# Selective scan: GpSimd's four products in slots 0, 3, 6 and 9 of a group, and the next group's preparation in other slots

## What is computed

```python
xz = x @ W_in
x_inner, z = jnp.split(xz, 2, axis=-1)
xc = jax.lax.conv_general_dilated(x_inner.swapaxes(1, 2), conv_w, ...) + conv_b[None, :, None]
xc = jax.nn.silu(xc.swapaxes(1, 2))
x_ssm = xc @ W_xproj
delta_raw, Bm, Cm = x_ssm[..., :1], x_ssm[..., 1:1 + D_STATE], x_ssm[..., 1 + D_STATE:]
delta = jax.nn.softplus(delta_raw * w_dt + b_dt)
A = -jnp.exp(A_log)
# selective scan over the sequence:
dA = jnp.exp(delta[..., None] * A)
dBx = delta[..., None] * Bm[:, :, None, :] * xc[..., None]
h = dA_t * h + dBx_t
y = jnp.einsum('bdn,bn->bd', h, c_t)
# after the scan:
y = y + xc * D_param
y = y * jax.nn.silu(z)
return y @ W_out
```

## Time and profile before

| what | value |
|---|---|
| median of three executions | 3499.23 us |
| the profiled execution | 3500.63 us, its span 3498.5 us |
| selective scan, from first to last scan | 2100.05 to 2581.5 us |
| one middle group, first scan to first scan | 61.4 us |
| VectorE busy in it | 55.3 us |
| TensorE, GpSimd, ScalarE busy in it | 51.0, 51.3, 32.1 us |

### The profile page before, as it was taken

How to read it: one execution, slowest core, us unless ns; L and a number is a source line. 1 busy time by engine, 2 the same in 40 slices (tenths; PEclk the granted TensorE clock), 3 DMA queues, 4 the chain that set the end, 5 groups by cost and what they waited for, 6 DMA issues and landing times. The chain is left out here.

```text
span 3498.5 us, 77906 instructions
## 1 busy us (share of the span) xinstructions
PE 2926.0 (84%) x23239; PEld 2004.9 (57%) x23239; DVE 2498.6 (71%) x7699; ACT 2017.0 (58%) x6248; POOL 1886.9 (54%) x1994
## 2 busy tenths in 40 slices
PE   7999698899998988679999978888772779869967
PEld 5769544567776876446777743333341447736645
DVE  7976767889997762448999958989876124457863
ACT  5545504789997553127888854545430225569954
POOL 4640202678886981445767748888840531127830
PEclk9999899999999999789999998999885889979989
DMA  3210002422221000221111123444330239800000
GB/s 110 87 40 0 7 1 72 132 82 86 86 87 51 1 7 20 72 64 33 36 38 37 37 74 132 141 136 141 134 141 3 35 68 241 198 8 1 2 7 24
DMA packets 142313, 233.86 MB, mean 67 GB/s; under 512 B 28652, under 2 KB 104718, under 8 KB 141431
## 3 DMA queue, kind: packets, MB, share of 16 engines
q1 hardware_dynamic: 133944, 221.59, 21.4%
q0 software_dynamic: 8128, 9.45, 1.5%
HBM read 200.42 MB, written 13.71 MB: 61 GB/s over the span
## 5 line engine op out<-in xcount | busy, mean ns | idle before, releaser
L3479 PE MATMUL l2a_pY<-l2a_hc,ident 128*128 128x512 f32 x512 | 275.3, 677 | 89.7 <-POOL l2a_hc L3398 55.5
L2705 POOL TENSOR_TENSOR l2x_att_prob<-l2x_att_prob,l2x_att_rs 128x1024 f32<-128x1024 f32 x128 | 242.3, 1893 | 134.6 <-DVE l2x_att_rs L2926 134.6
L3368 POOL TENSOR_TENSOR l2a_dbu<-l2a_dx,l2a_BC 128x1024 f32<-128x1024 f32 x128 | 298.6, 2354 | 21.2 <-PE l2a_pY L3479 10.6
L2876 ACT ACTIVATE l2x_att_prob<-l2x_att_prob,l2x_att_nmx 128x257 f32<-128x257 f32 x512 | 255.1, 500 | 81.0 <-DVE l2x_att_nmx L2921 80.9
L2705 POOL TENSOR_TENSOR l1x_att_prob<-l1x_att_prob,l1x_att_rs 128x1024 f32<-128x1024 f32 x128 | 242.3, 1893 | 76.1 <-DVE l1x_att_rs L2926 76.1
L3496 ACT ACTIVATE l2a_pA<-l2a_dl,l2a_A 128x512 f32<-128x512 f32 x256 | 174.5, 689 | 187.8 <-DVE l2a_pH L3602 112.1
L2876 ACT ACTIVATE l1x_att_prob<-l1x_att_prob,l1x_att_nmx 128x257 f32<-128x257 f32 x512 | 255.4, 502 | 25.9 <-DVE l1x_att_nmx L2921 23.1
L3479 PEld LDWEIGHTS l2a_pY<-l2a_hc,ident 128*128 128x128 f32 x512 | 103.6, 211 | 253.0 <-issue 120.4
L3602 DVE TENSOR_TENSOR_SCAN l2a_pH<-l2a_pA,l2a_dbu 128x512 f32<-128x512 f32 x192 | 224.8, 1216 | 23.2 <-POOL l2a_dbu L3368 12.2
L2921 DVE CUSTOM_DVE_ANT_0 l1x_att_prob<-l1x_att_pS,l1x_att_mask 128x257 f32<-128x257 f32 x512 | 192.4, 414 | 7.5 <-PE l1x_att_pS L2793 7.2
L2921 DVE CUSTOM_DVE_ANT_0 l2x_att_prob<-l2x_att_pS,l2x_att_mask 128x257 f32<-128x257 f32 x512 | 191.4, 412 | 3.4 <-PE l2x_att_pS L2793 3.0
(11 more groups left out here) (763 smaller groups left out, 8866.8 us busy)
## 6 DMA issues: line engine op xcount, KB each, us to landing
l2a_BC<-l2a_rows SPq DMA_DIRECT2D x128, 512.0 KB, 3.8
l3x_att_ctn<-ctx_n SPq DMA_DIRECT2D x32, 576.0 KB, 13.7
l0x_att_kvs<-ctx_t SPq DMA_DIRECT2D x32, 514.0 KB, 3.5
l1x_att_ctx<-ctx_t SPq DMA_DIRECT2D x128, 128.5 KB, 2.1
l1x_k_xin<-ctx_t SPq DMA_DIRECT2D x32, 514.0 KB, 3.5
l1x_att_kT<-l1x_KA SPq DMA_DIRECT2D x128, 128.5 KB, 2.2
l2x_att_ctx<-ctx_t SPq DMA_DIRECT2D x128, 128.5 KB, 2.1
l3x_att_ctx<-ctx_t SPq DMA_DIRECT2D x32, 514.0 KB, 11.8
```

What stands on the lines that cost most here:

```text
L2705: pool.tensor_tensor(p, p, bc(rs[:, b, :], 2, LAST), ALU.mult).then_inc(scaled, 1)
L2876: last = act.activation(prob[:, b, j, 0:KEYS], prob[:, b, j, 0:KEYS], ACT.Exp, bias=nmx[:, b, j:j + 1], scale=-1.0, accum_out=sums[:, b, j ...
L3368: pool.tensor_tensor(dbu[:, u % 3], dx[:, g % 2], bc(BC[:, u % RING, 0, :], 1, NC), ALU.mult).then_inc(dbu_made, 1)
L3479: last = pe.matmul(pY[c][:, :], env.ident[:, :], hc[:, u % 3, c, :], start=False, stop=n == NS - 1)
```

## The change

GpSimd's products go from slots 1, 5, 9, 13 to 0, 3, 6, 9. `dbu` and `hc` get a fourth buffer, and the increments run three units ahead. The pieces of the next group move:

| piece | slot before | slot after |
|---|---|---|
| convolution, first half | 1, 2 | 14, one group earlier |
| convolution, second half | 2, 3 | 0 |
| tanh (ScalarE) | 3, 4 | 0, 2 |
| `xc` (VectorE) | 4, 5 | 2, 3 |
| `w_bc`, `w_dt` (TensorE) | 5, 6 | 5, 4 |
| Abs, Exp, Ln (ScalarE) | 7, 9, 10 | 5, 6, 7 |
| copy of B and C, Relu (ScalarE) | 6, 8 | 8, 8 |
| `dl`, `dx` (GpSimd) | 11, 12 | 10, 11 |
| gate: `w_z`, tanh, `sz` | 8 and 10, 11 and 13, 12 and 14 | 9 and 10, 10 and 12, 11 and 13 |
| projection of the output, addition | 0, 1 | 12, 14 of the group after |

The two convolutions change banks of `pR`, and the output uses the other bank. For group 0 VectorE makes `dl`, `dx` and the first increments, which GpSimd made. The last projection and addition stand behind the loop.

```diff
-        dbu, hc = st.sb("dbu", [P, 3, NC, 512]), st.sb("hc", [P, 3, NC, 512])
+        dbu, hc = st.sb("dbu", [P, 4, NC, 512]), st.sb("hc", [P, 4, NC, 512])
...
+        dbu_first = st.sem("dbu_first")
...
         def on_pool(u):
-            return u % 4 == 1
+            return u % NS in (0, 3, 6, 9)
...
+        def product_ahead(u):
+
+            return max([k for k in range(u) if on_pool(k) == on_pool(u)], default=-1)
+
+        def increments_done(eng, u):
+            if u == 0:
+                eng.wait_ge(dbu_first, 1)
+            elif u > 0:
+                eng.wait_ge(dbu_made, u)
...
-                    done(pool, h_made, 2 * (u - 3) + 1)
+                    done(pool, h_made, 2 * (u - 4) + 1)
...
-                    if n == 11:
+                    if n == 10 and g:
...
-                    if n == 12:
+                    if n == 11 and g:
...
                     if n == 15 and g == 0:
-                        increments(0)
                         increments(1)
+                        increments(2)
 
                 def unit(u):
-                    if u + 2 < UNITS:
-                        increments(u + 2)
+                    if u + 3 < UNITS:
+                        increments(u + 3)
...
-                        done(pool, y_added, u - 3)
+                        done(pool, y_added, u - 4)
...
-                def convolved(g, c, taps, end=False):
+                def convolved(g, c):
...
+                    bank = pR[1 - c]
...
+                def projected(g):
+                    done(pe, ysz_made, 2 * g + 1)
...
                 def piece(g, n):
-                    if n == 0 and there(g - 2):
-                        done(pe, ysz_made, 2 * (g - 2) + 1)
-                        if there(g - 1):
-                            done(pe, sz_made, 2 * (g - 1) + 1)
...
+                    if n == 12 and there(g - 2):
+                        done(pe, sz_made, 2 * min(g, GROUPS - 1))
+                        projected(g - 2)
+                    if n == 0 and there(g):
+                        done(pe, added, g - 3)
+                        convolved(g, 1)
+                    if n == 14 and there(g + 1):
+                        done(pe, sz_made, 2 * g + 1)
+                        convolved(g + 1, 0)
...
-                    if n == 1:
-                        done(pe, sz_made, 2 * (g - 1))
...
-                    if n == 2:
...
-                    if n == 3:
-                        convolved(g, 1, (1, 2, 3), end=True)
+                    if n == 4:
+                        done(pe, xc_made, 2 * g + 1)
...
+                        last.then_inc(dt_made, 1)
                     if n == 5:
...
-                    if n == 6:
-                        for c in range(NC):
...
-                    if n in (8, 10):
-                        c = n // 2 - 4
+                    if n in (9, 10):
+                        c = n - 9
...
-                slots(piece, unit, 1)
+                convolved(0, 0)
+                slots(piece, unit, 0)
+                projected(GROUPS - 1)
...
-                    if n in (3, 4):
-                        c = n - 3
+                    if n in (0, 2):
+                        c = n // 2
...
-                    if n == 6:
-                        done(act, bc_made, g)
...
-                    if n == 7:
+                        act.activation(thx[:, c, :], pR[1 - c][:, :], ACT.Tanh).then_inc(thx_made, 1)
+                    if n == 5:
                         done(act, dt_made, g)
...
+                    if n == 6:
+                        for c in range(NC):
+                            done(act, ab_made, 2 * g + c)
+                            act.activation(lg[:, c, :], lg[:, c, :], ACT.Exp, scale=-1.0).then_inc(ex_made, 1)
...
+                    if n == 7:
+                        for c in range(NC):
+                            done(act, ex_made, 2 * g + c)
+                            act.activation(lg[:, c, :], lg[:, c, :], ACT.Ln, bias=env.ones[:, 0:1]).then_inc(lg_made, 1)
...
                     if n == 8:
+                        done(act, bc_made, g)
+                        if g:
+                            act.wait_ge(bc_stored, 16 * g)
+                        act.activation(bcs[:, :], pR[0][0:2 * NS, :], ACT.Copy).then_inc(bc_kept, 1)
...
-                    if n == 9:
-                        for c in range(NC):
-                            done(act, ab_made, 2 * g + c)
-                            act.activation(lg[:, c, :], lg[:, c, :], ACT.Exp, scale=-1.0).then_inc(ex_made, 1)
...
-                    if n in (11, 13):
-                        c = (n - 11) // 2
+                    if n in (10, 12):
+                        c = (n - 10) // 2
...
-                    if n == 10:
-                        for c in range(NC):
-                            done(act, ex_made, 2 * g + c)
-                            act.activation(lg[:, c, :], lg[:, c, :], ACT.Ln, bias=env.ones[:, 0:1]).then_inc(lg_made, 1)
...
-                    if n == 1 and there(g - 2):
-                        done(dve, out_made, g - 2)
...
+                    if n == 14 and there(g - 2):
+                        add(g - 2)
...
-                    if n in (4, 5):
-                        c = n - 4
+                    if n in (2, 3):
+                        c = n - 2
...
-                    if n in (12, 14):
-                        c = (n - 12) // 2
+                    if n == 10 and g == 0:
+                        done(dve, lg_made, 1)
+                        done(dve, rl_made, 1)
+                        dve.tensor_tensor(dl[:, 0], rl[:, :, :], lg[:, :, :], ALU.add).then_inc(dl_sum, 1)
+                        done(dve, dl_sum, 0)
+                        done(dve, xc_made, 1)
+                        dve.tensor_tensor(dx[:, 0], dl[:, 0], xc[:, 0], ALU.mult).then_inc(dx_made, 1)
+                        done(dve, dx_made, 0)
+                        dve.memset(dl[:, 0].rearrange("p c (b t) -> p (c b) t", t=S)[:, :, 0:1], BIG
+                                   ).then_inc(dl_made, 1)
+                        dve.wait_ge(landed[0], 16)
+                        dve.tensor_tensor(dbu[:, 0], dx[:, 0], bc(BC[:, 0, 0, :], 1, NC), ALU.mult
+                                          ).then_inc(dbu_first, 1)
+                    if n in (11, 13):
+                        c = (n - 11) // 2
                         done(dve, thz_made, 2 * g + c)
...
-                    done(dve, dbu_made, u)
+                    increments_done(dve, u)
...
-                        if on_pool(u):
-                            product_done(dve, u - 4)
-                            h = hh[:, c, :]
-                        else:
-                            product_done(dve, u - 2 if on_pool(u - 1) else u - 1)
-                            h = pH[c][:, :]
-                        dve.tensor_tensor_scan(h, pA[c][:, :], dbu[:, u % 3, c, :], 0.0, ALU.mult, ALU.add
+                        product_done(dve, product_ahead(u))
+                        h = hh[:, c, :] if on_pool(u) else pH[c][:, :]
```

More of the change, by code:

```diff
@@ L3335, in on_pool, with pool_products @@
         def on_pool(u):
-            return u % 4 == 1
+            return u % NS in (0, 3, 6, 9)
+        def pool_products(u):
+            return sum(1 for k in range(u + 1) if on_pool(k))
         def product_done(eng, u):
@@ L3418, in _ @@
                 pe.wait_ge(prep, 7)
-                def convolved(g, c, taps, end=False):
+                def convolved(g, c):
                     x = by_batch(env.XNT[:, g * 512:(g + 1) * 512])
-                    for s in taps:
-                        pe.matmul(by_batch(pR[c][:, :])[:, :, s:S], w_x[:, 3 - s, c * P:(c + 1) * P], x[:, :, 0:S - s],
+                    bank = pR[1 - c]
+                    for s in range(4):
+                        pe.matmul(by_batch(bank[:, :])[:, :, s:S], w_x[:, 3 - s, c * P:(c + 1) * P], x[:, :, 0:S - s],
@@ L3424, in convolved @@
                                   start=s == 0, stop=False)
-                    if end:
-                        pe.matmul(pR[c][:, :], cb[0:1, c * P:(c + 1) * P], env.ones[0:1, :], start=False, stop=True
-                                  ).then_inc(x_made, 1)
-                def piece(g, n):
-                    if n == 0 and there(g - 2):
-                        done(pe, ysz_made, 2 * (g - 2) + 1)
-                        if there(g - 1):
-                            done(pe, sz_made, 2 * (g - 1) + 1)
-                        for t in range(TG):
-                            for c in range(NC):
-                                last = pe.matmul(pR[1][:, t * D:(t + 1) * D], ysz[:, c, t * P:(t + 1) * P],
-                                                 w_out[:, c, :], start=c == 0, stop=c == 1)
-                        last.then_inc(out_made, 1)
+                    pe.matmul(bank[:, :], cb[0:1, c * P:(c + 1) * P], env.ones[0:1, :], start=False, stop=True
+                              ).then_inc(x_made, 1)
@@ new lines, in projected @@
```

(27 more changed lines are left out.)

41 lines of the change are left out of this document (20 added, 21 removed).

## The result

The changed kernel takes 3467.36 us (median of four, 3461.55 to 3469.83) against 3499.26 before: ratio 0.9912, 95% interval 0.9895 to 0.9929. That is faster by 32 us; 3469.5 was forecast. The profiled execution took 3469.83 us, its span 3467.7.

A forecast was written before the change was run, and what follows sets the result against it. VectorE was taken as the bound, busy 55.26 of 61.41 us per group. Terms 8.6 + 19.4 + 7.7 + 3.1 - 7.7 + 0.5 - 1.9 = 29.7 us took 3499.23 to 3469.5 us, range 3459 to 3489.

The forecast's parts named there:

- 1. *Increments.: Scans' wait for GpSimd's increments goes, by products before `dl` and `dx`, a fourth buffer, three units ahead: 8.6 us gained.
- 2. *`ysz`.: At group ends units 10 to 15 drain promptly on TensorE, so VectorE's `ysz` wait for `pY` goes: 19.4 us gained.
- The 0.1 us to spare: At a group end, TensorE finishes unit 15 at 11.4 and VectorE reaches `ysz` at 11.5, at full clock.
- the rival: TensorE late at group ends: at low clock ten to twenty more passes precede `ysz`; 3480 to 3490 us, chance 0.18 (shared).
- 3. *Tanh.: VectorE's `xc` wait for ScalarE's tanh goes, both convolutions being done by slot 1: 7.7 us gained.
- 4. *Direct pairs.: VectorE product pairs followed directly by a `pH` scan fall from seven to five per group: 3.1 us gained.
- 5. *ScalarE.: Late decays delay the scans of units 9 and 10 by 0.74 and 0.89 us per group: 7.7 us lost.
- The first wait: Unit 9's scan starts 0.74 us late, its decay delayed by the logarithms in slot 7.
- the second: Unit 10's scan starts 0.89 us late, copy and Relus standing together behind the delayed decay; may not come, 3461, 0.12.
- 6. *The start.: First group's operations on VectorE: first scan 2.4 us earlier, second pair after tanh 1.9 late; net 0.5 us gained.
- 7. *The clock.: TensorE loses clock behind 2.6 us gaps; before unit 3 this delays `w_dt` and a scan by 0.4: 1.9 us lost.

The follow-up runs named there:

- e11: The changed kernel with three buffers and increments two units ahead, as before the change: 3462.61 us, the scan 490.9 us.
- e3: The kernel before with only four buffers of `dbu` and `hc` and increments three units ahead: 3497.71 us, the scan 519.5 us.
- e2: The kernel before with only GpSimd's products moved to slots 0, 3, 6, 9: 3476.65 us, the scan 500.0 us.
- e1: The changed kernel with GpSimd's products back in slots 1, 5, 9, 13: 3495.94 us, the scan 525.9 us.
- e4: The kernel before with eight unused TensorE instructions (sixteen passes) in the gap before slot 13's product: 3486.95 us, the scan 509.0 us.
- e7: The changed kernel with four unused TensorE passes before the convolution of slot 14, at six group ends: 3483.26 us, the scan 499.8 us.
- e8: The changed kernel with ten unused TensorE passes at the one group end without a convolution: 3458.19 us, the scan 487.5 us.
- e5: The changed kernel with ScalarE's two Relus in slot 9 instead of 8: 3458.77 us, the scan 484.5 us.
- e6: The changed kernel with logarithms in slot 10, copy 7, Relus 8, gate tanh 9 and 12, `dl`, `dx` 12 and 13: 3450.49 us, the scan 479.0 us.
- e10: The changed kernel run again unaltered, for a second trace: 3472.50 us, the scan 490.4 us.
- e12: The changed kernel with the first group's `dl`, `dx` and first increments back on GpSimd: 3463.73 us (one execution), the scan 493.5 us.
- e9: e6 with the passes of e8, four unused passes in slot 12 of group 0, and group 0's gate before its logarithms: 3455.85 us, the scan 480.2 us.

## Why the prediction was right, point by point

The forecast gain was 29.7 us, the scan's is 30.6. A middle group gained 4.4 us on the mean (61.44 to 57.0); the terms that belong to it give 4.4 without that of the clock and 4.15 with it. The large terms (1 to 5) came by the mechanisms that were given for them, with half of the reason for point 1 wrong. That the small ones (6 and 7) end so near is luck: 7 was too large by 1.3 us, and a loss of 1.6 us that stood in no term took its place.

1. *Increments.* The wait went, 8.6 us as part of the whole. The reason given was half wrong: the fourth buffer and the third unit ahead do nothing in a middle group (e11), and removed alone the wait is worth nothing (e3). The slots, with three buffers, take it away (e2).
2. *`ysz`.* Right in cause for the slots (e1, e2): six of seven waits went. Two factors make the late drain, and the prediction counted them as one: the late product and the lost clock. With the clock held and the product as late, `ysz` doesn't wait (e4, every second group). The 0.1 us to spare, forecast for full clock, is 0.1 in the rows and 0.3 by e7. In the rival the convolution's passes were the danger; they end in time, and where they are missing the clock fell and 1.63 us were lost (e8).
3. *Tanh.* Right: the wait is gone in every group. No run takes this point or the next alone; both rest on the rows.
4. *Direct pairs.* Right: five in a group instead of seven, still 1.40 against 1.19.
5. *ScalarE.* The first wait is 0.66 idle, a step 0.74 too long, as computed; the second 0.68 and 0.76, where 0.89 was computed. e5 removes the second, e6 both, though the profile names other releasers for them.
6. *The start.* The term failed in size. The first scan is 3.2 us earlier (28.0 after the `A` operation instead of 31.2; only 2.0 earlier in e10) where 2.4 was forecast, the third pair is late by 2.36 instead of 1.9: net 0.8 for 0.5. But undone in the new order (e12, one trace) it is worth 3.1 to 4.1 us. The step overlooked is the path from GpSimd's second product (slot 3) over TensorE and Abs to the decay of unit 7, with the clock that TensorE loses behind the gap.
7. *The clock.* Right in mechanism, wrong in size. Gaps of 2.3 to 2.6 us stand before units 3 and 9. In three groups, the same three in e10, the clock fell behind the one before unit 3. A group where it held and one where it fell, first TensorE (unit 3, and `w_dt` of the second), then VectorE (the scans of units 6 and 7):

```profile
2168.97 1.98 PE L3491 MATMUL l2a_pY<-l2a_hc,ident 128*128 128x512 f32 x4 [2.34 <-POOL l2a_hc L3412]
...
2225.89 3.67 PE L3491 MATMUL l2a_pY<-l2a_hc,ident 128*128 128x512 f32 x4 [2.40 <-POOL l2a_hc L3412]
2229.39 1.88 PE L3466 MATMUL l2a_pR<-l2a_xc,l2a_w_dt_raw 128*128 128x512 f32 x4
```

```profile
2174.08 2.33 DVE L3626 TENSOR_TENSOR_SCAN l2a_hh<-l2a_pA,l2a_dbu 128x512 f32<-128x512 f32 x2
2176.32 2.32 DVE L3626 TENSOR_TENSOR_SCAN l2a_pH<-l2a_pA,l2a_dbu 128x512 f32<-128x512 f32 x2
...
2230.99 2.33 DVE L3626 TENSOR_TENSOR_SCAN l2a_hh<-l2a_pA,l2a_dbu 128x512 f32<-128x512 f32 x2
2233.43 2.35 DVE L3626 TENSOR_TENSOR_SCAN l2a_pH<-l2a_pA,l2a_dbu 128x512 f32<-128x512 f32 x2
```

Where it fell, `w_dt` ended 21.3 us after the group's first scan instead of some 19.7, and the scan of unit 7 came 2.44 behind that of unit 6 instead of 2.24. These 0.2 us are the steps of 57.1 beside those of 56.9; the waits view does not list them. So a scan lost 0.2 where 0.4 was assumed, three times in place of 7 x 2/3: 0.6 us for 1.9. (Twelve passes at full clock took 5.3 us in e4, so the 7.11 us of the earlier trace rows are 1.8 too long, not 1.7.) The 1.63 us at the last but one group end, in no term, come on top.

## What to carry to other kernels

A wait's price in the waits view is what it costs only if nothing later on the same engine waits for something that doesn't move (e3): price waits from the last to the first, and check by removing one alone. The view can leave small delays out and name the wrong releaser, so compare the steps of equal groups too. Where one in-order engine feeds another, put its late work where the consumer has slack (e2); at the start of a stage, where GpSimd worked without a pause, the waits removed ahead of it came back further on (e9). Where TensorE's idle gaps cost it its clock, work put into them is cheaper than none (e4, e8), up to the spare time (e7).
